# First attention of a hybrid layer stack: query tiles in alternating order, passes written out, and an instruction order of their own for small tiles

## What is computed

```
q = (h @ Wq).reshape(s, 16, 192); rope on the last 64 of each head     # s = 2048, h: 2048 x 256
scores = einsum('qhd,khd->hqk', q, k) / sqrt(192) + minimum(causal, top_k_mask)
attn = softmax(scores)
out = einsum('hqk,khd->qhd', attn, v) @ Wo
```

## Time and profile before

| | |
|---|---|
| time, median of 3 runs | 3481.03 us (3480.75 to 3494.99) |
| profiled execution | 3483.64 us, its span 3482.0 us |
| first attention, first score to last weigh | 950.48 to 2199.58 us of the span: 1249.10 us |
| TensorE busy in it | 1172.23 us |
| VectorE, ScalarE busy in it | 921.79 and 725.40 us |
| granted TensorE clock in it | 0.99 of full speed |

### The profile page before, as it was taken

One profiled execution on the slowest core, in us unless ns is written; L12 is line 12 of the kernel. 1 busy time (PEld: TensorE's weight loads), 2 busy tenths in 40 slices (PEclk: granted clock), 3 DMA queues, 4 the chain that ended last, 5 costly groups with the idle time before them and its releaser, 6 DMA issues. The chain is left out here.

```text
span 3482.0 us, 45060 instructions
## 1 busy us (share of the span) xinstructions
PE 2622.4 (75%) x12496; PEld 1651.7 (47%) x12497; DVE 2087.5 (60%) x4677; ACT 1584.9 (46%) x2875; POOL 465.3 (13%) x758
## 2 busy tenths in 40 slices
PE   5991069601689989998999999588249999997693
PEld 2330023201467767775777677455124444444452
DVE  3338953598267767775777777532317776763422
ACT  2446324660256555664655566223112666664231
POOL 0220012100011111101111110031300000000314
PEclk8555555555699999999999999789675999998797
DMA  3000000001300000000000000222270022000123
GB/s 98 0 0 0 0 0 0 0 0 39 110 10 7 7 9 9 7 6 11 7 7 7 10 7 1 73 80 78 67 172 8 2 37 37 1 1 2 61 82 100
DMA packets 82226, 100.62 MB, mean 29 GB/s; under 512 B 24931, under 2 KB 71619, under 8 KB 79043
## 3 DMA queue, kind: packets, MB, share of 16 engines
q1 hardware_dynamic: 69476, 70.45, 7.8%
q0 software_dynamic: 12544, 27.68, 2.5%
HBM read 60.99 MB, written 36.70 MB: 28 GB/s over the span
## 5 line engine op out<-in xcount | busy, mean ns | idle before, releaser
L1122 ACT ACTIVATE aa_pt_hi<-psum 128x512 fp32r<-128x512 f32 x544 | 322.3, 595 | 343.5 <-PE psum L1028 342.8
L1662 DVE TENSOR_REDUCE ab_part_max<-psum 128x1 f32<-128x512 f32 (+3 forms) x640 | 364.2, 607 | 177.4 <-PE psum L1500 172.7
L1184 DVE TENSOR_TENSOR aa_pt_lo<-psum,aa_pt_hi 128x512 fp32r<-128x512 f32 x544 | 368.1, 687 | 39.6 <-ACT aa_pt_hi L1122 38.8
L1604 ACT ACTIVATE ab_prob<-psum 128x512 f32<-128x512 f32 (+3 forms) x640 | 303.5, 537 | 165.3 <-PE psum L1529 161.9
L1171 DVE CUSTOM_DVE_ANT_0 aa_prob<-psum,bias 128x512 f32<-128x512 f32 (+2 forms) x480 | 284.1, 597 | 108.1 <-PE psum L1018 102.4
L1500 PE MATMUL psum<-ab_k_stack,ab_q_stack 49*128 49x512 f32 (+3 forms) x640 | 285.4, 489 | 26.4 <-DVE ab_part_max L1662 25.8
L973 POOL TENSOR_TENSOR aa_tmp<-aa_q_nat,rope 128x128 f32<-128x128 f32 x256 | 109.1, 458 | 1294.7 <-ACT aa_q_nat L1099 1294.7
L1016 PE MATMUL psum<-ka_hi,aa_q_hi 128*128 128x512 f32 (+3 forms) x640 | 272.9, 426 | 9.2 <-DVE aa_chunk_max L1171 8.0
L1039 PE MATMUL psum<-aa_pt_hi,c_stack 128*128 128x512 f32 x544 | 271.5, 499 | 2.6 <-DVE aa_pt_lo L1184 2.6
L1028 PE MATMUL psum<-ident,aa_prob 128*128 128x128 f32 x1600 | 264.7, 273 | 10.2 <-ACT aa_prob L1114 5.6
L504 PE MATMUL psum<-ix_bad_row,mean 128*128 128x1 f32 x4 | 1.2, 363 | 340.9 <-DVE ix_bad_row L631 340.9
(11 more groups left out here) (343 smaller groups left out, 4980.7 us busy)
## 6 DMA issues: line engine op xcount, KB each, us to landing
f_rows_in<-sent SPq DMA_DIRECT2D x80, 128.0 KB, 2.0
done<-f_rows_out POOLq DMA_DIRECT2D x80, 128.0 KB, 2.0
aa_xt<-xT_rows SPq DMA_DIRECT2D x64, 128.0 KB, 2.4
w<-in_w SPq DMA_DIRECT2D x6, 896.0 KB, 7.2
sent<-ixp_zeros SPq DMA_DIRECT2D x4, 1280.0 KB, 10.4
x<-in_hidden SPq DMA_DIRECT2D x2, 2048.0 KB, 9.1
ab_q_stack<-stash_q_hi SPq DMA_DIRECT2D x32, 128.0 KB, 9.9
ab_k_stack<-stash_k_hi SPq DMA_DIRECT2D x32, 128.0 KB, 11.2
```

Of the source, the lines that this page charges most:

```text
L1122: nc.scalar.activation(pt_hi[(TB[t] + j) % RING][:], turn_bank[(TB[t] + j) % RING], ACT.Copy).then_inc(pt_hi_done, 1)
L1184: nc.vector.tensor_tensor(pt_lo[ring][:], turn_bank[(TB[t] + j) % RING], pt_hi[ring][:].bitcast(F32), ALU.subtract).then_inc(pt_lo_done, 1)
L1604: nc.scalar.activation(prob[i % 2][h][:, 0:w], t_bank[slot % RING][:, 0:w], ACT.Exp).then_inc(t_taken, 1)
L1662: nc.vector.tensor_reduce(part_max[e % 2][:, 4 * h + t % 4, part:part + 1], s_bank[piece % 2][:, 0:w], AX.X, ALU.max).then_inc(s_used, 1)
```

## The change

Within a pass the tiles are taken in the order 8, 7, 9, 6, 10, 5, 11, 4, 12, 3, 13, 2, 14, 1, 15, 0: a *large* tile (8 to 15) at each even position, a *small* one (0 to 7) at each odd one. Buffers and counters go by position, data by `TILE[position]`. All four passes are written out on TensorE, ScalarE and VectorE, and the `y` of a pass's last tile moves into the first step of the next pass. In the step of a small tile, `turn` comes in the first 0.6 of it and each `weigh` 0.28 behind its `turn`, the scores (of the next, large tile) are spread over 0.9 instead of 0.75 of the step, and `flip` stands at 0.8 instead of 0.4. `keep` goes into ScalarE's list behind the last `weigh`, three places late, instead of at its end.

```
+FLIP_LATE, LARGE_BY, TURNS_BY, WEIGH_AFTER = 0.8, 0.9, 0.6, 0.28
...
-    chunks = [(t + 4) // 4 for t in range(NT)]
+    HALF_NT = NT // 2
+    TILE = [HALF_NT + p // 2 if p % 2 == 0 else HALF_NT - 1 - p // 2 for p in range(NT)]
+    chunks = [(tile + 4) // 4 for tile in TILE]
...
+            t, todo = g % NT, []
+            blocks = TILE[t] + 1
+            scored, flipped, queried = (g + n < NG * NT for n in (1, 2, 3))
+            small = t % 2 == 1
+            for j in range(blocks):
+                if small:
+                    at = TURNS_BY * (j + 0.3) / blocks
+                    todo += [(at, ("turn", j)), (at + WEIGH_AFTER, ("weigh", j))]
+                else:
+                    todo += [(j / blocks, ("turn", j)), ((j + LAG) / blocks + 2e-6, ("weigh", j))]
...
-                    todo.append(((k + 0.5) / n * SCORES_BY, ("score", *divmod(k, chunks[(t + 1) % NT]))))
+                    todo.append(((k + 0.5) / n * (LARGE_BY if small else SCORES_BY), ("score", *divmod(k, chunks[(t + 1) % NT]))))
             if flipped:
-                todo.append((FLIP_AT, ("flip",)))
+                todo.append((FLIP_LATE if small else FLIP_AT, ("flip",)))
...
-            with eng.Fori(0, NG - 1) as i:
-                passes(i, False)
-            passes(NG - 1, True)
+            for g in range(NG * NT):
+                ahead = [divmod(g + n, NT) for n in (1, 2, 3)]
+                step(*divmod(g, NT), ahead, divmod(g - 1, NT), plan(g))
+            finish(NG - 1)
...
-                    for what in behind(steps, {"project": 0, "flip": 0, "score": 4, "turn": 0}):
+                    for what in behind(steps, {"project": 0, "flip": 0, "score": 4, "turn": 0, "weigh": 3}):
```

More of the change, by code:

```diff
@@ L861, in attention_a @@
     NG = HA // GH
-    chunks = [(t + 4) // 4 for t in range(NT)]
+    HALF_NT = NT // 2
+    TILE = [HALF_NT + p // 2 if p % 2 == 0 else HALF_NT - 1 - p // 2 for p in range(NT)]
+    chunks = [(tile + 4) // 4 for tile in TILE]
     QB = [GH * sum(chunks[:t]) for t in range(NT + 1)]
-    TB = [t * (t + 1) // 2 for t in range(NT + 1)]
+    TB = [sum(tile + 1 for tile in TILE[:t]) for t in range(NT + 1)]
     QN, TN = QB[NT], TB[NT]
@@ L874, in attention_a @@
         q_lo = [sb(f"q_lo{p}", [P, GH * P], F32R) for p in range(2)]
-        prob = [[sb(f"prob0{h}", [P, S - P])[:] for h in range(GH)],
-                [xT[:, h, :] for h in range(KC)] + [sb(f"prob1{h}", [P, S])[:] for h in range(KC, GH)]]
+        prob = [[xT[:, h, :] for h in range(KC)] + [sb(f"prob0{h}", [P, S])[:] for h in range(KC, GH)],
+                [sb(f"prob1{h}", [P, HALF_NT * P])[:] for h in range(GH)]]
         pt_hi = [sb(f"pt_hi{n}", [P, GH * P], F32R) for n in range(RING)]
@@ L909, in attention_a, with plan @@
         y_bank = q_bank = bank[7]
[L911 to L919, removed]
+        def plan(g):
+            t, todo = g % NT, []
[8 more added lines that the diff above has]
+                    todo += [(j / blocks, ("turn", j)), ((j + LAG) / blocks + 2e-6, ("weigh", j))]
+            if g:
                 todo += [(Y_AT[pair], ("y", pair)) for pair in range(GH // 2)]
@@ L934, in behind, with walk @@
             return [what for _, _, what in sorted(mine)]
[L936 to L944, removed]
+        def walk(before, step, finish):
             before()
-            with eng.Fori(0, NG - 1) as i:
-                passes(i, False)
-            passes(NG - 1, True)
+            for g in range(NG * NT):
+                ahead = [divmod(g + n, NT) for n in (1, 2, 3)]
+                step(*divmod(g, NT), ahead, divmod(g - 1, NT), plan(g))
+            finish(NG - 1)
         with nc.Block() as block:
@@ L955, in load @@
                     sp.wait_ge(q_proj, g + 1)
-                    sp.dma_start(xt[t % 2][:], xT_rows[:, :, t * P:(t + 1) * P]).then_inc(xt_in[t % 2], 16)
+                    sp.dma_start(xt[t % 2][:], xT_rows[:, :, TILE[t] * P:(TILE[t] + 1) * P]).then_inc(xt_in[t % 2], 16)
                 with sp.Fori(0, NG) as i:
@@ L966, in rotate @@
                     g = i * NT + t
-                    cos = rope[:, 0, t, :].unsqueeze(1).to_broadcast([P, GH, HALF])
-                    sin = rope[:, 1, t, :].unsqueeze(1).to_broadcast([P, GH, HALF])
+                    cos = rope[:, 0, TILE[t], :].unsqueeze(1).to_broadcast([P, GH, HALF])
+                    sin = rope[:, 1, TILE[t], :].unsqueeze(1).to_broadcast([P, GH, HALF])
                     r1, r2 = q_nat[:, :, RANK:RANK + HALF], q_nat[:, :, RANK + HALF:]
@@ L1009, in score @@
                     g, n = i * NT + t, i * QN + QB[t] + h * chunks[t] + c
-                    w = min(CH, (t + 1) * P - c * CH)
+                    w = min(CH, (TILE[t] + 1) * P - c * CH)
                     if h == 0 and c == 0:
@@ L1038, in weigh @@
                         pe.wait_ge(kept, g + 1)
-                    nc.tensor.matmul(out[:], c_stack[:, j, :], pt_hi[ring][:], start=j == 0, stop=j == t,
+                    nc.tensor.matmul(out[:], c_stack[:, j, :], pt_hi[ring][:], start=j == 0, stop=j == TILE[t],
                                      skip_group_check=True)
-                    nc.tensor.matmul(out[0:RANK, :], c_stack[:, j, 0:RANK], pt_lo[ring][:], start=False, stop=j == t,
+                    nc.tensor.matmul(out[0:RANK, :], c_stack[:, j, 0:RANK], pt_lo[ring][:], start=False, stop=j == TILE[t],
                                      skip_group_check=True).then_inc(pv_done, 1)
@@ L1069, in before, with step @@
                     for h in range(GH):
-                        score(0, 0, h, 0)
-                def step(i, t, ahead, steps):
+                        for c in range(chunks[0]):
+                            score(0, 0, h, c)
+                def step(i, t, ahead, behind, steps):
                     for what in steps:
@@ L1084, in step @@
                         else:
-                            leave(i, t - 1, what[1])
+                            leave(*behind, what[1])
                 def finish(i):
@@ L1089, in finish @@
                         leave(i, NT - 1, pair)
-                walk(pe, before, step, finish)
+                walk(before, step, finish)
             @block.scalar
@@ L1108, in exponentials @@
                 def exponentials(i, t, h):
-                    g, L = i * NT + t, (t + 1) * P
+                    g, L = i * NT + t, (TILE[t] + 1) * P
                     act.wait_ge(max_ready, g * GH + h + 1)
@@ L1139, in before, with step @@
                         exponentials(0, 0, h)
-                def step(i, t, ahead, steps):
-                    for what in behind(steps, {"project": 0, "flip": 0, "score": 4, "turn": 0}):
+                def step(i, t, ahead, _, steps):
+                    for what in behind(steps, {"project": 0, "flip": 0, "score": 4, "turn": 0, "weigh": 3}):
                         if what[0] == "project":
@@ L1148, in step @@
                             split_turned(i, t, what[1])
+                        elif what[0] == "weigh":
+                            if what[1] == TILE[t]:
+                                keep(i, t)
                         elif what[2] == chunks[ahead[0][1]] - 1:
                             exponentials(*ahead[0], what[1])
-                    keep(i, t)
-                walk(act, before, step, lambda i: None)
+                walk(before, step, lambda i: None)
             @block.vector
@@ L1172, in take @@
                                                    score_bank[(QB[t] + h * chunks[t] + c) % 2][:, 0:w],
-                                                   bias[:, TRI[t] + c * CH:TRI[t] + c * CH + w], 1.0, -BIG, ALU.add, ALU.max,
+                                                   bias[:, TRI[TILE[t]] + c * CH:TRI[TILE[t]] + c * CH + w], 1.0, -BIG, ALU.add, ALU.max,
                                                    chunk_max[t % 2][:, h, c:c + 1]).then_inc(scores_out, 1)
@@ L1193, in invert @@
                     dve.wait_ge(total_turned, g + 1)
-                    nc.vector.tensor_scalar(inv[t % 2][:], inv[t % 2][:], filled[:, t:t + 1], None,
+                    nc.vector.tensor_scalar(inv[t % 2][:], inv[t % 2][:], filled[:, TILE[t]:TILE[t] + 1], None,
                                             ALU.mult).then_inc(inv_done, 1)
@@ L1202, in add @@
                         dve.wait_ge(x_added, g * GH + h + 4 * GH)
-                        nc.vector.scalar_tensor_tensor(out=x[:, t, :], in0=y_bank[:, h % 2 * D:(h % 2 + 1) * D],
-                                                       scalar=inv[t % 2][:, h:h + 1], in1=x[:, t, :],
+                        nc.vector.scalar_tensor_tensor(out=x[:, TILE[t], :], in0=y_bank[:, h % 2 * D:(h % 2 + 1) * D],
+                                                       scalar=inv[t % 2][:, h:h + 1], in1=x[:, TILE[t], :],
                                                        op0=ALU.mult, op1=ALU.add).then_inc(x_added, 1)
@@ L1220, in before, with step @@
                     for h in range(GH):
-                        take(0, 0, h, 0)
```

(8 more changed lines are left out.)

## The result

| | before | after |
|---|---|---|
| time, median | 3480.89 us (4 runs) | 3577.61 us (3572.42 to 3578.28, 4 runs) |
| ratio | | 1.0266, 95% interval 1.0246 to 1.0285 |
| profiled span | 3482.0 us | 3576.6 us |
| first attention | 950.48 to 2199.58: 1249.10 us | 949.69 to 2287.35: 1337.66 us |

What follows compares the result with a forecast made beforehand. TensorE's own work was taken to bound the kernel. Stall of 151.2 us against 132.3 made it 19 us slower, the clock 44 more: 3481 + 63 = 3544 us, the forecast's own range 3505 to 3585.

Steps and rivals of the forecast that it cites:

- The work doesn't change: First attention stage: TensorE's own work, 1116.8 us over four passes, is the same in any order of tiles.
- The gap before `turn` 0: End of a small step: TensorE idles through the projection's copy, then the last head's exponentials; mean 2.6 us a step.
- The example of tile 3: Tile 3's step scoring tile 13, worked through to time the end of a small step; earliest `project` 0.8 us late.
- the formula: TensorE's gap before `turn` 0: about 0.04 + 0.49 + e + 0.23 us, with exponentials e of 1.25 to 2.00.
- The flip's copy: End of a small step: the copy stands behind exponentials on ScalarE, making `project` late by 0.9 us.
- Two banks: Small steps: up to 16 scores packed on two score banks wait for them, 0.75 us a step.
- The whole small step: Stall of a step on tiles 0 to 7: 0.9 + 2.6 + 0.75 = 4.25 us, bounds 2.4 and 6.1.
- the prices of the forecast: TensorE work times from distances of starts: block 0.91 us, 512-wide score 0.69, `y` 0.86, `project` 1.72, `flip` 0.44.
- The large steps: Steps on tiles 8 to 15, now scoring a small tile: 0.4 us of stall each, 12.8 us over 32.
- the clock: Half clock in the large step behind a small step's gap: 22 of 31 places at 2.0 us, 44 us.
- Passes written out: Unlooped passes: the loop's ends vanish, and fetching code that runs once is priced at nothing.

Runs made afterwards that it cites:

- the filled gap: Changed kernel with eight idle matmuls behind the projection of each small step; 3538.02 us, ratio 1.0174 to the kernel before.
- the late copy: Changed kernel with the projection's copy moved behind the last exponentials in ScalarE's list of a small step; 3498.06 us, ratio 1.0017 to the kernel before.

## Why the prediction was right, and where it was off

The direction and the mechanism held; the time, 3577.6, is 34 us above the forecast and inside the range. By its steps:

- *The work doesn't change.* Held: as many matmul records in the stage.
- *The gap before `turn` 0*, 31 x 2.6 = 81 us: measured 81.5 in 32 waits. One of these is the prologue's (2.1 us) and one the last, where no projection is left and the gap is 4.7; the other 30 hold 74.7 us, 2.5 each. The example of tile 3 came at 2.46 us where the formula gives 2.54. That its cure is the order of copy and exponentials was shown by moving that one item.
- *The flip's copy*, 31 x 0.9 = 28 us: 19.2 measured. The wait was foreseen, its reason only in part. The copy was to stand behind large exponentials; in the trace it starts some 0.1 us or less after the flip's end at 23 of the 31 ends, 0.35 us after it ahead of tile 11 and 1.25 us only ahead of tile 15. The rest of the wait is the way from the flip through both copies to the projection, 1.5 us, which in the example two scores cover for 1.1. This wait could also not be had back by an earlier flip.
- *Two banks*, 31 x 0.75 = 23 us: 19.9 of waits, 12 more than before.
- *The whole small step*, 4.25 us: 5.00, taken over 32 steps as 684.4 us less 524.3 of work by the prices of the forecast. This is the term that was mis-sized, by 26 us over all of them, as much as the whole miss in the stage (88.6 against 63). In the second pass it runs from 3.7 us (tile 7) to 6.4 (tile 1). 10.8 us of it is the flip waiting for VectorE's adds of the `y`, which the forecast left out. Some 25 to 30 us are in no listed wait; waits under 0.15 us are not listed, and which engine causes them stays open.
- *The large steps*, 0.4 us, and *the clock*, 44 us: together 57, measured together 55.0, but that the sum fits is luck. Without the falls large steps stall 29.1 us, 0.9 each and not 0.4, which is 16 us more than forecast, and the falls cost 25 us by the filled gap and 26 by the late copy, 18 less than forecast. Their number was nearly right, 22 forecast and 20 measured (the expectations say 18). Their price wasn't: 2.0 us of lost clock were put down for each, 1.7 were lost, and 1.1 to 1.6 us of time in the pairs of steps compared above, since part of the half clock lies over waits.
- *Passes written out*: forecast at nothing beside the vanished loop ends. Those ends, with the falls behind them, were worth 17 us in the stage (20 and 25 by the two ratios), not to be seen in the result because the rest of the change loses over 100.
- 6 us lie behind the stage, at a clock lower by 0.01 in code that the change doesn't touch. That is within what profiles scatter by: the part behind the stage takes 1282.4 us before and 1289.2 after, and in three experiments on one chip 1286.7, 1288.1 and 1296.3, with the same code there.

No run of the changed kernel itself on the chips of the experiments was made; its ratio and theirs are each to the kernel before beside them.

## What to carry to other kernels

When a list of work is ordered by hand, follow the longest chain over the end of each step through *every* engine's list: an item that waits for a late producer (here a copy behind a projection) holds up all that is queued behind it, however ready that is. Moving it a place or two was worth 87 us, and moving the flip ahead of it earlier was worth nothing, because other waits took its place. A gap that comes back in each step can cost twice on TensorE, once as idle time (here 56 us) and once as half clock in the dense work behind it (here 25).

## What the runs showed of the hardware

Gaps of 1.9 to 2.7 us on TensorE, with a projection and a gap of 0.2 to 1.2 us ahead of it, were followed by the half clock at 19 of 30 places, for 3.4 us each, and not at the others, though the same gap of the same tile had it in one pass and not in the next. With the gaps at those places cut to 1.5 us at most (late copy), or filled to 0.9 at most (idle matmuls), it came at none of the 30. Matmuls whose result nobody reads, put into the gap, kept the clock at 1.00 and made the stage 24 us shorter and the kernel some 32 us faster.
